# Half-row masks, half-width values, transposed factors and a split softmax in a 16-head transformer kernel, with every instruction queue ordered anew

## The reference

```python
x = x + four_layers(layernorm(x), ctx[:, :32 keys that matter], itok)   # rmsnorm, causal attention of 16 heads of 8
                                                                     # with rope, masked cross attention, gated MLP
x = x + factor_attention(layernorm(x), u, v)    # 16 channels of 64: sigmoid(qu qv^T) applied both ways, times u and v
x = x + layernorm(x) @ (weight + folded disha)
x = x + perceiver(ctx of 1601 keys, layernorm(x), mask)              # 2 heads of 64, masked softmax over 1601 + 64 keys
x = x + causal_attention(layernorm(x))                               # 16 heads of 8, rope
x = x + top2_of_8_experts(layernorm(x))                              # 128 -> 512 -> 128, relu
```

## Time and profile before

| | |
|---|---|
| median of 3 runs | 533.04 us (532.92 to 533.9) |
| the profiled execution | 531.21 us, span 529.2 us, mean granted clock 0.981 |
| TensorE busy | 478.1 us, 5383 records (weight loads 406.3 us) |
| VectorE, ScalarE, GpSimd busy | 373.4, 242.6, 229.7 us |
| DMA | 27.05 MB, mean 51 GB/s |

### The profile page before, as it was taken

One profiled execution on the slowest core, in us unless ns is written; L12 is line 12 of the kernel. 1 busy time (PEld: TensorE's weight loads), 2 busy tenths in 40 slices (PEclk: granted clock), 3 DMA queues, 4 the chain that ended last, 5 costly groups with the idle time before them and its releaser, 6 DMA issues.

```text
span 529.2 us, 14124 instructions
## 1 busy us (share of the span) xinstructions
PE 478.1 (90%) x5383; PEld 406.3 (77%) x5398; DVE 373.4 (71%) x1016; ACT 242.6 (46%) x623; POOL 229.7 (43%) x345
## 2 busy tenths in 40 slices
PE   0699999999999989949999998999999988799997
PEld 0577786778678766938777778899999975689997
DVE  5386688668866876646978879878787787543454
ACT  0246645653665466503333266556555633522221
POOL 3682168117713661135893321788777224100000
PEclk9899999999999999979999999999999999879999
DMA  7700111012019000021123231012100000000000
GB/s 213 272 13 3 36 28 54 9 32 79 1 40 370 11 2 2 1 83 56 65 66 126 72 119 62 2 63 63 66 1 1 2 2 1 1 1 1 1 11 10
DMA packets 10030, 27.05 MB, mean 51 GB/s; under 512 B 1426, under 2 KB 4839, under 8 KB 9703
## 3 DMA queue, kind: packets, MB, share of 16 engines
q1 hardware_dynamic: 9958, 26.09, 14.7%
HBM read 25.82 MB, written 0.26 MB: 49 GB/s over the span
## 4 chain that ended last, share of the span: by engine, by line
PE 48%; DVE 3%; ACT 2%; issue 2%; POOL 0%; DVEq 0%; ACTq 0%
PE sc L1440 3%; PE sc L1356 3%; PE sc L1345 3%; PE pt L1430 2%; PE sc L1371 2%; PE sc L1430 2%; PE sc L1256 2%; PE sc L1264 2%; PE pt L1371 2%; PE sc L1296 1%; PE pt L1296 1%; PE sm L1440 1%; PE sc L1275 1%; PE sm L1430 1%; PE sc L1339 1%
## 5 line engine op out<-in xcount | busy, mean ns | idle before, releaser
L869 POOL TENSOR_TENSOR rstd<-ss,par 128x1 f32<-128x1 f32 x52 | 28.6, 550 | 103.0 <-ACT sq L712 103.0
L729 ACT ACTIVATE pr<-sd 128x1024 f32<-128x1024 f32 (+1 forms) x36 | 31.1, 864 | 7.9 <-DVE sd L781 7.0
L1240 POOL TENSOR_TENSOR xh<-xh,rsx 128x512 f32<-128x512 f32 (+1 forms) x32 | 31.4, 982 | 4.6
L1236 POOL TENSOR_TENSOR xh<-cx,mvx 128x512 f32<-128x512 f32 (+1 forms) x32 | 28.4, 889 | 0.8
L1215 DVE BATCH_NORM_STATS2 stx<-cx 128x6 f32<-128x128 f32 x104 | 22.7, 275 | 4.4 <-DMA cx<-ctx_in 4.4
L763 DVE TENSOR_SCALAR h<-y,rstd 128x128 f32<-128x128 f32 x48 | 23.5, 490 | 3.3 <-POOL rstd L869 3.3
L712 ACT ACTIVATE sq<-y 128x129 f32<-128x129 f32 x52 | 16.2, 311 | 18.4 <-DVE y L813 17.4
L1776 POOL TENSOR_SCALAR rk<-kss 128x8 f32<-128x8 f32 (+1 forms) x32 | 7.5, 236 | 38.0 <-DVE kss L1652 36.6
L855 POOL TENSOR_TENSOR qk<-rope 128x256 f32<-128x256 f32 x20 | 14.6, 728 | 19.1 <-DVE rope L767 19.1
L863 POOL TENSOR_TENSOR kblk<-qk,cf 128x512 f32<-128x512 f32 x20 | 20.8, 1041 | 0.9
L1756 POOL TENSOR_TENSOR rstd<-mv,par 128x1 f32<-128x1 f32 x21 | 5.1, 244 | 36.7 <-DVE mv L1592 26.8
(11 more groups left out here) (587 smaller groups left out, 1542.4 us busy)
## 6 DMA issues: line engine op xcount, KB each, us to landing
cx<-ctx_in SPq DMA_DIRECT2D x13, 768.0 KB
we<-we_in SPq DMA_DIRECT2D x8, 514.0 KB, 9.0
wc<-wc_in SPq DMA_DIRECT2D x4, 768.5 KB, 5.8
wa<-wa_in SPq DMA_DIRECT2D x5, 387.0 KB, 3.0
wb<-wb_in SPq DMA_DIRECT2D x4, 256.5 KB, 4.1
uvT<-uvT_in SPq DMA_DIRECT2D x1, 1024.0 KB, 4.9
uv<-uv_in SPq DMA_DIRECT2D x1, 1024.0 KB, 6.9
cx<-ctx_in SPq DMA_DIRECT2D x13, 32.5 KB
```

The lines of the kernel that those rows point to most:

```text
L729: nc.scalar.activation(pr[:, t, 0:k], sd[:, t, 0:k], ACT.Exp).then_inc(s[piece], 1)
L869: nc.gpsimd.tensor_tensor(rstd[:, t:t + 1], ss[:, t:t + 1], par[:, 1:2], ALU.pow).then_inc(s[piece], 1)
L1236: nc.gpsimd.tensor_tensor(part, cx[u % 2][:, tiles, :], mvx[:, b, tiles, 0].unsqueeze(2).to_broadcast(shape), ALU.subtract).then_inc(xm["c ...
L1240: nc.gpsimd.tensor_tensor(part, part, rsx[:, b, tiles].unsqueeze(2).to_broadcast(shape), ALU.mult).then_inc(xm["c_normed"], 1)
```

## The change

- `values` computes for each half of the output rows only the 64 columns that this half uses (the weight's columns are sorted by the parity of the head), and `vblk` becomes two copies of half the rows instead of one product with a mask.
- The causal mask's constants stand in both row halves; the two mask products of `causal` use 64 rows each, the first the upper, the second the lower half; `cmask` likewise.
- `max`, `shift`, `exp`, `turn`, `turned` and `weigh` are split in two pieces of 512 columns (a and b).
- `along0/1` are eight transposes each of what uT0/1 took out, and un0/1 plain copies; uT0/1 of the next tile wait for along.
- `c_scores` writes the mask products of a group first and then the score products.
- Zeroing of vblk and vcblk and the copy to mem4 go from GpSimd to ScalarE in the first block.
- All places of both tables are new, and the places behind the layers have a start for each tile or sequence instead of a constant step. Some semaphores are merged. Row scaling (norm1 to norm3) stays on VectorE.

What the new order puts where, by the sort: in the layers, `kc` of a layer stands on GpSimd between k_groups, base and pow2 of the same layer instead of before pow1; the softmax pieces of one tile stand between those of its neighbours. Behind the layers, tile 0's last attention starts among the context's steps (causal.0 before the scores of sequence 6, turna.0 and weigha.0 before the last sum_ctx), tiles 2 and 3 have theirs between up_e and down_e of the first half of experts. Before, all four tiles' turn_o and out stood ahead of the first up_e.

```diff
-PERIOD, SKEW = 82.56, (0.0, 5.95, 11.55, 17.21)
+PERIOD, SKEW = 94.96, (0.0, 6.64, 13.36, 19.85)
...
+YWAY = {"HEAD": (-56.19, -25.95, 7.73, 36.57),
+        "XWAY": (64.27, 84.49, 105.74, 127.53, 152.47, 175.97, 199.94, 223.58),
+        "TAIL": (162.31, 201.10, 271.55, 346.92),
+        "HALF": (298.32, 541.98),
...
-            nc.gpsimd.memset(vblk[:], 0.0).then_inc(s["zeroed"], 1)
-            nc.gpsimd.memset(vcblk[:], 0.0).then_inc(s["zeroed"], 1)
-            pool.wait_ge(s["mem_loaded"], 16)
-            nc.gpsimd.tensor_copy(mem4[:], memT[:].unsqueeze(2).to_broadcast([P, B, 4, KF])).then_inc(s["mem4_ready"], 1)
...
+            for blocks in (vblk[:].rearrange("p t b j a e -> p (t b j a e)"), vcblk[:].rearrange("p b g i e -> p (b g i e)")):
+                nc.scalar.activation(blocks, par[:, 2:3].to_broadcast([P, B * 4 * 4 * 9]), ACT.Copy, scale=0.0).then_inc(s["zeroed"], 1)
+            act.wait_ge(s["mem_loaded"], 16)
+            nc.scalar.copy(mem4[:], memT[:].unsqueeze(2).to_broadcast([P, B, 4, KF])).then_inc(s["zeroed"], 1)
...
-                        last = nc.tensor.matmul(bank[L * a:L * a + L, 512 + P * b:512 + P * b + P], hT[:, t, L * b:L * b + L],
-                                                A[:, A_V:A_V + P], start=True, stop=True)
+                        last = nc.tensor.matmul(bank[L * a:L * a + L, 512 + L * b:512 + L * b + L], hT[:, t, L * b:L * b + L],
+                                                A[:, A_V + L * a:A_V + L * a + L], start=True, stop=True)
...
-                nc.tensor.matmul(bank[:, 0:512], causal, it64, start=True, stop=True)
                 pe.wait_ge(s["vblk"], n)
-                nc.tensor.matmul(bank[:, 512:1024], causal, it64, start=True, stop=True)
+                for k in range(2):
+                    rows = slice(L * k, L * k + L)
+                    nc.tensor.matmul(bank[:, 512 * k:512 * k + 512], causal[rows, :], it64[rows, :], start=True, stop=True)
...
-                    nc.tensor.matmul(bank[:, 512 * p:512 * p + 256], cmask[:, P * t:P * t + P], it32, start=True, stop=True)
+                    rows = slice(L * p, L * p + L)
+                    nc.tensor.matmul(bank[:, 512 * p:512 * p + 256], cmask[rows, P * t:P * t + P], it32[rows, :], start=True, stop=True)
...
-                nc.vector.tensor_tensor(
-                    vblk[:, t, :, :, :, 0:8].rearrange("p b j a d -> p (b j) a d"),
-                    held(od, "project", l, t)[:, 512:768].rearrange("p (j a d) -> p j a d", a=2, d=8),
-                    vm2.unsqueeze(1).unsqueeze(3).to_broadcast([P, 16, 2, 8]), ALU.mult).then_inc(s["vblk"], 1)
+                for a in range(2):
+                    rows = slice(L * a, L * a + L)
+                    last = nc.vector.tensor_copy(vblk[rows, t, :, :, a, 0:8].rearrange("p b j d -> p (b j) d"),
+                                                 held(od, "project", l, t)[rows, 512:640].rearrange("p (j d) -> p j d", d=8))
+                last.then_inc(s["vblk"], 1)
...
-                pe.wait_ge(s["uv_loaded"], 48)
-                x_wait(pe, "z_turned", i + 1)
-                for j in range(2):
-                    last = nc.tensor.matmul(bank[:, 512 * j:512 * j + 512], hT[:, i, :], uvT[:, w, 512 * j:512 * j + 512], start=True, stop=True)
+                x_wait(pe, "uT%d" % w, i + 1)
+                for j in range(8):
+                    last = nc.tensor.transpose(bank[:, P * j:P * j + P], ut[:, w, j, :], ident)
...
-                    part = bank[:, P * j:P * j + P]
-                    nc.tensor.matmul(part, notm[:, P * c:P * c + P], sel[:, i, :], start=True, stop=True)
-                    last = nc.tensor.matmul(part, xnT[n % 3][:, P * j:P * j + P], qp(i),
+                    nc.tensor.matmul(bank[:, P * j:P * j + P], notm[:, P * c:P * c + P], sel[:, i, :], start=j == 0, stop=True, skip_group_check=True)
+                for j, c in enumerate(CG[g]):
+                    last = nc.tensor.matmul(bank[:, P * j:P * j + P], xnT[n % 3][:, P * j:P * j + P], qp(i),
                                             start=False, stop=True, skip_group_check=True)
...
```

More of the change, by code:

```diff
@@ new lines @@
+    "PE": {"memory": -64.59, "turn1": -13.11, "project": -10.22, "values": -6.14, "causal": 2.03, "scores": 5.56,
+           "turna": 12.76, "turnb": 13.31, "weigha": 13.92, "weighb": 17.55, "turn_o": 19.75, "out": 23.58,
+           "turn2": 29.41, "qc": 30.73, "cmask": 32.39, "cscores": 32.79, "cturn": 42.97, "cweigh": 44.68,
+           "cturn_o": 48.60, "cout": 50.09, "turn3": 56.78, "gate": 59.64, "up": 63.08, "down": 70.36},
+    "ACT": {"square1": -20.64, "mem_k": -49.09, "hT1": -12.87, "q_groups": 1.68, "expa": 9.15, "expb": 11.49,
+            "turneda": 11.78, "turnedb": 14.73, "oT": 21.01, "square2": 23.16, "hT2": 28.16, "qcT": 30.38,
+            "cexp": 37.80, "cturned": 41.68, "coT": 47.08, "square3": 49.40, "hT3": 55.45, "tanh": 60.63},
@@ L78 @@
 HOLDS = {
-    1: {"memory": ("mem_k", "mem_v"), "turn1": ("hT1",), "weigh": ("o",), "turn_o": ("oT",), "out": ("y1",), "turn2": ("hT2",),
+    1: {"memory": ("mem_k", "mem_v"), "turn1": ("hT1",), "turna": ("turneda",), "turnb": ("turnedb",), "weigha": ("o",), "turn_o": ("oT",), "out": ("y1",), "turn2": ("hT2",),
         "qc": ("qcT",), "cturn": ("cturned",), "cweigh": ("co",), "cturn_o": ("coT",), "cout": ("y2",), "turn3": ("hT3",),
         "down": ("y3",)},
-    2: {"project": ("shift",), "cmask": ("cshift",), "gate": ("hidden",), "turn": ("turned",)},
+    2: {"project": ("shifta", "shiftb"), "cmask": ("cshift",), "gate": ("hidden",)},
 }
@@ L85 @@
 BEHIND = "cturn_o cout turn3 gate up down coT square3 hT3 tanh y2 norm3 gated hidden y3 pow3".split()
-SELF = ("turn1 project values causal scores turn weigh turn_o out hT1 q_groups exp turned oT rope vblk max shift recip o y1 "
+SELF = ("turn1 project values causal scores turna turnb weigha weighb turn_o out hT1 q_groups expa expb turneda turnedb oT rope vblk "
+        "maxa maxb shifta shiftb recip o y1 "
         "rope_sum rope_bias k_groups").split()
```

239 lines of the change are left out of this document (128 added, 111 removed).

## The result

| | before | after |
|---|---|---|
| median of 4 runs, us | 532.98 (531.03 to 533.9) | 513.74 (512.5 to 514.93) |
| ratio, 95% interval | | 0.9643 (0.9605 to 0.9682) |
| profiled execution / its span, us | 531.21 / 529.2 | 514.56 / 512.8 |
| TensorE's first product, us from the start | 14.76 | 12.56 |
| from that product to the end of the last down, the four layers | 212.1 | 211.0 |

What follows compares the result with a forecast made beforehand. The prediction took TensorE's work, with a thin margin of latency, to bound the layers. Its terms, -2.5 -0.6 -4.0 -9.8 -9.0 +1.0 = -24.9 us, gave 506.3 for the profiled execution and 508.0 as median, range 496 to 523.

Steps and rivals of the forecast that it cites:

- (b): Layers: shape steps between halves and quarters cost nothing, waits shrink by 2.2 us each; 498 us, chance 0.17.
- (d): Causal and cmask: the two mask halves don't overlap, +6.0 us; 514 us, chance 0.08.
- (c): Softmax: the halves make TensorE wait for ScalarE's exp or turned, up to 2.1 us a tile; 536 us, chance 0.05.
- (a): Whole kernel: new places bring nothing and waits stay, only work is saved; 521 us, chance 0.18.
- Start, -2.5: Before TensorE's first product: zeroing on ScalarE speeds VectorE's normalisation, -2.1 us; kc no longer ahead of pow1, -0.4.
- Layers' work, -0.6: TensorE's work in the layers: -8.4 us from values and masks, +7.8 from 56 more shape changes.
- Layers' waits, -4.0 from the halves: Layers: softmax in halves shortens each tile's path, waits fall 1.0 us a layer; bounds +6 and -9.
- The bound of +6: Layers: upper bound in us on the change in waits, as the new order has more places to wait in.
- Behind the layers, work -9.8: TensorE's work after the layers: along -6.8 us, context masks -3.8, cmask -1.7, 14 more shape changes +2.5.
- Along, +1.0 not realised, bounds -3 and +6: Factor attention: along must wait for uT, so 1 us of the 6.8 saved by transposes is lost.
- Masks first, -3.8: Context stage: four masks in a row save 0.16 us in each of 24 groups, if masks stay at 0.055 each.
- All places anew, -9: Last attention: its idle and half-clock time, 14 us in all, is filled with expert products; bounds -4 and -13.

Runs made afterwards that it cites:

- the unsplit kernel: Changed kernel with max, shift, exp, transposes, copies and weigh in one piece each, at the second half's place: 524.75 us, ratio 0.9832.
- old places, one piece: Changed kernel with the four layers in the order from before the change and the softmax unsplit: 515.66 us, ratio 0.9659.
- The addition experiment: Changed kernel with one more VectorE reduction ahead of each of the 32 sums of the context keys: 517.73 us, ratio 0.9723.

## Why the prediction was right, and where it was off

*Right in range and direction*, and the sizes of the single parts were: values 0.38; causal's second product hidden; along 0.88; masks in a row 1.17; first product at 12.56 (said 12.7); clock 1.0 at the start of the experts; the shape changes at their full price (cscores right behind cmask take 0.59 us, 0.45 of them their own steps; from column to row halves 0.11), so rivals (b) and (d) were rightly not taken, though the time is the 514 of (d). The Trainium skill, TensorEngine Tiling (Array Packing), Key Properties, has a change of the tiling mode drain the engine; with 0.14 us from row halves to quarters the trace agrees that these two are different modes. (c), ScalarE exposed, did not come in after, but its mechanism is the 1.29 us of the unsplit kernel. (a), work only, was the nearest rival for the layers.

*Start, -2.5*: -2.2.

*Layers' work, -0.6*: -0.6 in the sum, but the reading of it was wrong. "Layers are bound by TensorE's work, with a thin margin of latency" is the step that failed. 3.4 us of waits in 50.8 look like a margin, and taking work away hardly reaches through them: 5.5 us less gave 0.5 (old places, one piece; 0.4 of 1.4 in a middle layer). Work that is added does: 2.1 more gave 1.4 (masks on all rows). I read from this that work and the chains of the tiles bound the layers together, each a little above the other in turn; the kernel in one piece differs from the one before in VectorE's work too, so this is argued and not isolated. A busy in-order queue with few gaps is no proof that its work is the bound, since what is taken off can come back as a wait.

*Layers' waits, -4.0 from the halves*: -0.4 in after. The mechanism exists (3.2 and 8.4 us), but it was booked against the old order, and the change brings another one, which without halves costs 7.8 us more and with them still 2.7, nearly all in the last layer. The middle layers did give 0.6 each of the 1.0; the last layer took most of it back. I had sorted the new queue only to count its changes of shape; a look at what stands between scores, turn and weigha there would have shown that the new order spends the shortened path instead of saving it. The bound of +6 that I gave for "more places to wait in" was the term that mattered.

*Behind the layers, work -9.8*: -9.7. *Along, +1.0 not realised, bounds -3 and +6*: 3 by the experiment, a mis-sized term. Which wait takes it (the path through uT, or VectorE) was not taken apart. *Masks first, -3.8*: the work is there, 0.9 comes through in the medians and at most 2.1 in the trace.

*All places anew, -9*: the tail's waits fell by 8.6, of which up to 5 are a stretch of 10 us at the lower clock that after doesn't have. But the price stands elsewhere: tile 0's softmax and the start of tile 1's were moved into the context stage, whose waits rose from 2.9 to 7.1. I had named VectorE above 90% there as what would make the prediction wrong, which came (91%), and put it only into the bounds of the -9. The addition experiment makes more work on VectorE a price of a quarter to two fifths. That it explains the 4.2 us is not shown: by the records of after TensorE waits there 1.2 us for VectorE (1.6 before), 0.5 for GpSimd and 2.7 for ScalarE (none before), and 1.7 of these are one wait at 314 us, 65 us ahead of tile 0's project:

```profile
312.51 0.46 ACT L1497 ACTIVATE hT<-sm,xw 128x128 f32<-128x128 f32 x1 [1.94 <-PE sm L1336]
...
314.10 1.13 PE L1368 MATMUL sm<-xw,xnT 128*128 128x128 f32 x8 [1.69 <-ACT xnT L1516]
```

The copy of the turned context keys (xnT) stood in ScalarE's queue behind one (hT) that waited for TensorE's own l_turn. That is a matter of two queues' order and not of VectorE's load.

In sum, of the 8.5 us of span that are missing 3.6 are the layers' waits, 4.2 the context stage's, and 0.7 the rest.

## What to carry to other kernels

Price a new order with the work it comes with and without it: here a path-shortening edit (halves) and a new order were each read as a gain in the layers, and there the second only spent the first. Read the stages one repetition at a time, the last one too: a sum over four layers hid that only the last had become longer. When an in-order queue is 95% busy, test whether its work bounds it by giving it less or more of it before booking savings at par; a wait in it may be stepped over only if the piece moved ahead was ready before the wait and the piece put off has no close successor.

## What the runs showed of the hardware

- Two products on the two row halves of the array, on different banks, overlap wholly: the pair of 512 columns takes 0.39 us by its record span, one alone 0.38. A change into or out of such a shape costs about what the others cost: 0.11 us into causal, 0.14 from cmask into quarters, 0.20 into the whole products of project.
- In the factor attention of twelve of the fourteen traces TensorE stands still once, for 0.7 to 1.65 us (eight times for 1.0 or more), within a group of 64 products, where the program has no wait ("issue" is time in which the engine waited for nothing that the profile shows). In after:

```profile
248.72 1.11 PE L1298 MATMUL sc<-sd 64*64 64x64 f32 x63
251.49 0.27 PE L1298 MATMUL sc<-sd 64*64 64x64 f32 x1 [1.65 <-issue]
```

  Its cause is open.
- In after one stretch is left at the lower level of the clock (1.2 GHz): it lies over the pause of 7.5 us that TensorE makes at the barrier and the first 6 us of work behind it. With the last attention filled, the one before the experts is gone. Two kernels with a longer context stage have another one between 420 and 450 (0.89 and 0.94, against 1.00), and eight have one of 3.4 to 6.8 us in the factor attention, which neither before nor after has; what brings these is open. The stretch of after:

```profile
220.00:240.00 20.00, 11.93 (x78) 11.24 (x77) 8.54 (x26) 3.92 (x14) 6.71 (x21) 0.74 0.27 91
```
